# Preloading the final pass's constants and first spectrum, and storing repeated map rows one image later, in a two-layer spectral convolution kernel

## The reference

```python
# layer 0: spectral convolution, 4 heads of 16 channels
x_freq = rfft2(gn(x))
core = einsum('bhixy,hioxy->bhoxy', xf[..., :32, :17], weight[..., :32, :17])
x = x + irfft2(core placed in zeros) + bias
# layer 1: normalisation on the hyperboloid, over all images and pixels
m = mean of gn(x) over batch and pixels, one vector of 64 channels
mu = m / sqrt(max(m0^2 - sum(m[1:]^2), EPS))
alpha = max(x0 * mu0 - x[1:] @ mu[1:], 1 + EPS);  d = arccosh(alpha)
var = mean(d * d);  coef = d / sqrt(alpha^2 - 1)
v = coef * (x - alpha * mu);  vo = v - v0 / (1 + mu0) * (mu + e0)
s = gamma * vo[1:] / (sqrt(var) + EPS) + beta;  t = sqrt(1 + sum(s * s))
x = x + concat([t, s])
```

## Time and profile before

| | before |
|---|---|
| median of 3 runs | 3675.0 us (3665.37 to 3679.16) |
| the profiled execution's own time | 3669.49 us |
| its span | 3667.9 us |
| busy share PE, DVE, ACT, POOL | 80%, 75%, 57%, 41% |
| mean granted TensorE clock | 0.886 of full speed |
| DMA | 1211.32 MB, mean 330 GB/s |

### The profile page before, as it was taken

One profiled execution on the slowest core, in us unless ns is written; L12 is line 12 of the kernel. 1 busy time (PEld: TensorE's weight loads), 2 busy tenths in 40 slices (PEclk: granted clock), 3 DMA queues, 4 the chain that ended last, 5 costly groups with the idle time before them and its releaser, 6 DMA issues. The chain is left out here.

```text
span 3667.9 us, 70122 instructions
## 1 busy us (share of the span) xinstructions
PE 2923.4 (80%) x26018; PEld 1461.4 (40%) x26018; DVE 2747.2 (75%) x2984; ACT 2096.8 (57%) x2866; POOL 1512.5 (41%) x862
## 2 busy tenths in 40 slices
PE   6998888989843766776775498898888899888887
PEld 3555555555521221222221344444444444444443
DVE  1888888888886546544564398888888888888888
ACT  5776676767720011101111388787777787777787
POOL 0101011010111111111111287787777777777778
PEclk9998888988866888887787699999999999999999
DMA  9877767777716989999996599999999999999998
GB/s 379 298 265 258 277 244 290 258 277 274 248 64 224 400 326 391 400 397 387 403 399 221 177 391 382 380 376 374 371 368 368 368 378 376 370 381 373 370 386 341
DMA packets 293210, 1211.32 MB, mean 330 GB/s; under 512 B 35266, under 2 KB 49799, under 8 KB 210695
## 3 DMA queue, kind: packets, MB, share of 16 engines
q1 hardware_dynamic: 263526, 1152.42, 82.5%
q0 software_dynamic: 14112, 43.37, 3.6%
q10 hardware_dynamic: 15360, 12.60, 1.2%
HBM read 883.89 MB, written 324.31 MB: 329 GB/s over the span
## 5 line engine op out<-in xcount | busy, mean ns | idle before, releaser
L1309 POOL TENSOR_TENSOR c_ot<-c_ot,c_pp 128x1024 f32<-128x1024 f32 x512 | 1213.6, 2372 | 411.2 <-DVE c_ot L1262 410.0
L1252 DVE SCALAR_TENSOR_TENSOR c_xt<-c_xt,keep_k,c_p_u 128x1024 f32<-128x1024 f32 x512 | 653.7, 1277 | 135.8 <-PE c_p_u L1132 109.5
L1262 DVE SCALAR_TENSOR_TENSOR c_ot<-c_p_f,keep_k,c_xt 128x1024 f32<-128x1024 f32 x512 | 657.3, 1284 | 108.3 <-DMA out<-c_ot 59.8
L1206 ACT ACTIVATE c_pp<-c_p_p,keep_cols 128x1024 f32<-128x1024 f32 x512 | 570.7, 1115 | 259.8 <-PE c_p_p L1144 258.7
L1132 PE MATMUL c_p_u<-c_mv,c_zc 64*128 64x256 f32 x4096 | 595.6, 410 | 78.9 <-DVE c_xt L1252 76.9
L1213 ACT ACTIVATE c_sq<-c_xt,keep_cols 128x1024 f32<-128x1024 f32 x512 | 583.1, 1139 | 63.9 <-DVE c_xt L1252 63.6
L330 ACT ACTIVATE a_junk<-a_xt 128x1024 bf16<-128x1024 f32 x512 | 537.1, 1053 | 29.1 <-DMA a_xt<-in_x 21.8
L249 PE MATMUL a_p_rows<-a_xt,a_dft_h 128*64 128x512 f32 x2048 | 516.3, 650 | 32.8 <-DMA a_bias_t<-in_bias 18.1
L1132 PEld LDWEIGHTS c_p_u<-c_mv,c_zc 64*128 64x128 f32 x4096 | 361.1, 190 | 362.7 <-issue 219.5
L528 POOL TENSOR_TENSOR a_sm<-a_sm 128x8 f32<-128x8 f32 x16 | 26.7, 1670 | 929.4 <-DVE a_sm L463 929.4
L1144 PE MATMUL c_p_f<-c_rt,keep_lw 64*128 64x512 bf16 x1024 | 315.3, 388 | 104.6 <-DVE c_ot L1262 95.8
(11 more groups left out here) (206 smaller groups left out, 2964.1 us busy)
## 6 DMA issues: line engine op xcount, KB each, us to landing
a_xt<-in_x SPq DMA_DIRECT2D x256, 1024.0 KB, 8.1
b_xt<-in_x SPq DMA_DIRECT2D x128, 2048.0 KB, 16.8
c_xt<-in_x SPq DMA_DIRECT2D x256, 1024.0 KB, 15.9
out<-c_ot SPq DMA_DIRECT2D x256, 1024.0 KB, 16.3
c_rt<-maps SPq DMA_DIRECT2D x256, 96.0 KB
maps<-b_maps ACTq DMA_DIRECT2D x192, 64.0 KB, 13.7
maps<-b_maps POOLq DMA_DIRECT2D x64, 192.0 KB, 10.0
dmap<-b_dmap POOLq DMA_DIRECT2D x16, 768.0 KB, 13.2
```

The lines of the kernel that those rows point to most:

```text
L1206: S.activation(pp[n][:], p_p[:], ACT.Identity, bias=keep["cols"][:, b, 1:2]).then_inc(pp_done, 1)
L1252: V.scalar_tensor_tensor(out=u, in0=u, scalar=kc, in1=p_u[:], op0=ALU.mult, op1=ALU.add).then_inc(u_done, 1)
L1262: V.scalar_tensor_tensor(out=ot[t % NB][:, at], in0=p_f[:], scalar=kinv, in1=xt[t % NB][:, at], op0=ALU.add, op1=ALU.mult).then_inc(f_done, 1)
L1309: P.tensor_tensor(o, o, pp[n][:], ALU.add).then_inc(o_done, 1)
```

## The change

In the second pass ACT's order becomes copy_z(b), repeat_maps(b-1), distances(b), with the last image's stores at the end. At the end of the second pass SP waits until DVE has done `combine` for all images, and loads image 0's spectrum, `idft_c` and the cosine table into tiles that are now in `keep`. The table in HBM is 64 rows high and four times as wide, so one load of 64 rows fills half of a `mv` tile, and `mv` is not zeroed any more. The kept `ys` tile also serves as DVE's scratch (`v1`, `v2`) at the start of the second pass; two memsets of the upper halves of `ys` and `idft` follow there, ahead of `dense(0)`. `misc` is loaded once. In the final pass TensorE and ACT wait for the PSUM bank's memset alone (`filled` 1) and the preload's semaphores; `hw` is awaited only before the first `sums`. The `rt` tiles are zeroed by DVE (two) and POOL (two), and SP issues the first two x tiles before it waits for them.

```diff
@@ -70,11 +70,11 @@
     scale = np.where(ky == 0, 1.0, 2.0)[:, None] / N
-    iw = np.zeros((48, W))
+    iw = np.zeros((64, W))
...
     iw[M2 + 2] = 1.0
-    c["idft_w"] = iw
+    c["idft_w"] = np.tile(iw, (1, 4))
@@ -586,7 +586,7 @@
         xt = [sb(f"xt{k}", [128, TB]) for k in range(NX)]
-        misc = sb("misc", [128, 24])
+        misc = keep["misc"]
@@ -599,7 +599,8 @@
         ac, lc, q2, q3, dsum = sb("ac", [128, B]), sb("lc", [128, B]), sb("q2", [128, B]), sb("q3", [128, B]), sb("dsum", [128, B])
-        v1, v2 = sb("v1", [128, B, C]), sb("v2", [128, B, C])
+        ys_flat = keep["ys"][:].rearrange("p c m -> p (c m)")
+        v1, v2 = (ys_flat[:, B * C * k:B * C * k + B * C].rearrange("p (b c) -> p b c", c=C) for k in range(2))
@@ -637,7 +638,7 @@
             sp.dma_start(idft_h[0:64], cst["idft_d"]).then_inc(c_in, 16)
-            sp.dma_start(idft_w[:], cst["idft_w"][0:YS]).then_inc(c_in, 16)
+            sp.dma_start(idft_w[:], cst["idft_w"][0:YS, 0:W]).then_inc(c_in, 16)
@@ -650,6 +651,14 @@
                     load(b, t)
+            sp.wait_ge(v_ready, 3 * B)
+            sp.wait_ge(uw_out, 16)
+            for half in range(2):
+                load_modes_0(sp, keep, spec, half)
+            sp.dma_start(keep["idft"][0:64].rearrange("p a b c -> p (a b c)"), cst["idft_c"]).then_inc(keep["pre_in"], 16)
+            for m in keep["mv"]:
+                for at in range(2):
+                    sp.dma_start(m[64 * at:64 * at + 64], cst["idft_w"]).then_inc(keep["pre_in"], 16)
@@ -743,13 +752,15 @@
                 copy_z(b)
+                repeat_maps(b - 1)
                 distances(b)
-                repeat_maps(b)
...
             act.wait_ge(setup, 4)
-            entry(0)
+            copy_z(0)
+            distances(0)
...
                 entry(b)
+            repeat_maps(B - 1)
@@ -958,6 +969,8 @@
             combine(1)
+            ch.inc(V.memset(keep["ys"][64:128], 0.0))
+            ch.inc(V.memset(keep["idft"][64:128], 0.0))
@@ -984,6 +997,12 @@
+def load_modes_0(sp, keep, spec, half):
+    for k in range(2):
+        sp.dma_start(keep["ys"][KX * k:KX * k + KX, 32 * half:32 * half + 32].rearrange("k (h i) m -> k h (i m)", h=2),
+                     spec[0, k].rearrange("(h k) n -> k h n", h=HEADS)[:, 2 * half:2 * half + 2]).then_inc(keep["ys_in"][half], 16)
@@ -999,8 +1018,8 @@
     r_in = [sem(f"r_in{k}") for k in range(NB)]
-    ys_in = [sem(f"ys_in{k}") for k in range(2)]
-    c_in, zeroed, filled = sem("c_in"), sem("zeroed"), sem("filled")
+    ys_in, pre_in = keep["ys_in"], keep["pre_in"]
+    zeroed, filled = sem("zeroed"), sem("filled")
@@ -1013,15 +1032,14 @@
         rt = [sb(f"rt{k}", [128, TC], BF16) for k in range(NB)]
-        mv = [sb(f"mv{k}", [128, 4 * W]) for k in range(NB)]
+        mv = keep["mv"]
         zc = [sb(f"zc{k}", [128, 32, 2 * C]) for k in range(2)]
-        ys = sb("ys", [128, C, YS])
+        ys = keep["ys"]
...
         arg, th, o0 = (sb(n, [128, 512]) for n in ("arg", "th", "o0"))
-        idft = sb("idft", [128, 2, 2, 64])
-        misc = sb("misc", [128, 24])
+        idft, misc = keep["idft"], keep["misc"]
@@ -1030,8 +1048,6 @@
         def _(sp):
-            sp = Sync(sp, c_in)
@@ -1089,17 +1105,10 @@
-            sp.wait_ge(zeroed, 2 * NB + 1)
-            for half in range(2):
-                load_modes(0, half)
-            sp.dma_start(idft[0:64].rearrange("p a b c -> p (a b c)"), cst["idft_c"]).then_inc(c_in, 16)
-            sp.dma_start(misc[:], cst["misc"]).then_inc(c_in, 16)
-            for m in mv:
-                for at in range(2):
-                    sp.dma_start(m[64 * at:64 * at + 48].rearrange("p (r w) -> p r w", w=W), cst["idft_w"].unsqueeze(1).to_broadcast((48, 4, W))).then_inc(c_in, 16)
...
                 load_x(0, t)
-            sp.wait_ge(c_in, 16 * (2 + 2 * NB))
+            sp.wait_ge(pre_in, PRE_IN)
+            sp.wait_ge(zeroed, NB)
@@ -1149,8 +1158,11 @@
                 pe.wait_ge(sq_done, b * GR + 2 * t + 2)
-                if t == 0 and not is_at(b, 0):
-                    pe.wait_ge(t_read, b)
+                if t == 0:
+                    if is_at(b, 0):
+                        pe.wait_ge(filled, 2)
+                    else:
+                        pe.wait_ge(t_read, b)
@@ -1173,8 +1185,8 @@
-            pe.wait_ge(c_in, 16 * (2 + 2 * NB))
-            pe.wait_ge(filled, 3)
+            pe.wait_ge(pre_in, PRE_IN)
+            pe.wait_ge(filled, 1)
@@ -1229,8 +1241,7 @@
-            act.wait_ge(zeroed, 2 * NB + 1)
-            act.wait_ge(filled, 3)
+            act.wait_ge(filled, 1)
@@ -1281,15 +1292,10 @@
-            for r in rt:
-                V.memset(r[:], 0.0).then_inc(zeroed, 1)
-            for m in mv:
-                V.memset(m[:], 0.0).then_inc(zeroed, 1)
-            V.memset(ys[:], 0.0).then_inc(zeroed, 1)
-            V.memset(idft[64:128], 0.0).then_inc(filled, 1)
...
             V.memset(hw[:], 0.0).then_inc(chain, 1)
-            dve.wait_ge(c_in, 16 * (2 + 2 * NB))
+            for r in rt[:2]:
+                V.memset(r[:], 0.0).then_inc(zeroed, 1)
@@ -1321,10 +1327,14 @@
+            for r in rt[2:]:
+                P.memset(r[:], 0.0).then_inc(zeroed, 1)
...
+
+PRE_IN = 16 * 9
@@ -1341,7 +1351,10 @@
             keep = {"lw": sb("lw", [128, B, C, 2], BF16), "cols": sb("cols", [128, B, 2]),
-                    "k": sb("k", [128, 4])}
+                    "k": sb("k", [128, 4]), "ys": sb("ys", [128, C, YS]), "idft": sb("idft", [128, 2, 2, 64]),
+                    "misc": sb("misc", [128, 24]), "mv": [sb(f"mv{k}", [128, 4 * W]) for k in range(4)],
+                    "ys_in": [ctx.enter_context(nc.semaphore(f"ys_in{k}")) for k in range(2)],
+                    "pre_in": ctx.enter_context(nc.semaphore("pre_in"))}
```

## The result

| | before | after |
|---|---|---|
| median | 3670.6 us (4 runs, 3665.4 to 3679.2) | 3796.4 us (4 runs, 3791.5 to 3800.0) |
| profiled execution, its span | 3667.9 us | 3797.5 us |
| busy share PE, DVE, ACT, POOL | 80, 75, 57, 41% | 78, 72, 55, 40% |

The changed kernel is slower: ratio 1.0339, 95% interval 1.0312 to 1.0367, or 126 us. In the profiled executions it is 129.6 us.

The account below looks back on a forecast made before the run. The second pass was taken as bound by both full DMA engines and a DVE-POOL loop. Terms +146 + 2.3 - 8 - 25.8 = +114.5 on 3669.5 gave 3784 us, range 3635 to 3840.

Parts of the forecast that it names:

- turn = 29.2 + D: Second pass, from one `dense` to the next: 29.2 us plus D, rising from 51.7 to 63 us, +146 over 13 turns.
- D: Time of POOL's queue from first map store to the spectrum's landing; forecast to rise from 22 to 34 us.
- the turning point: The D, put at 24.4 us, at which 13 longer turns lose the 31.5 us that the seams give.
- the seams: Effects outside the 13 turns: +2.3 us before the loop, -8 at the second pass's end, -25.8 at the final pass's start.
- The head start of POOL's stores: Second pass: POOL's stores start 0 to 5 us before x loads resume, saving 0 to 8 us of D.
- TensorE's new wait: Second pass: TensorE stands for `combine` instead of ACT's copy, some 15 us an image.
- s + 40 and s + 62: Times after s, the start of `dense(b-1)`: the next image's tile 5 lands, and its row transform can start.
- The end of the pass: End of the second pass: `dense(15)` starts 32 us after `dense(14)`, not 39.6, held by ACT's last stores: -8 us.
- The preload: Loads at the second pass's end cost 0; the final pass's first transform starts 25.8 us earlier.
- A: Rival: bytes bound the second pass, so D stays at 22 and the turn at 51.7; 3638 or 3626 us; chance 0.16.
- B: Rival: ACT's copy still falls behind something long enough for x loads to pause as now; 3638 us; chance 0.06.
- C: Rival: x loads resume late, TensorE staying at 1.2 GHz; D is 25 to 26, 3681 us; chance 0.08.

Follow-up runs that it names:

- experiment 4: Changed kernel with each x tile of the second pass loaded by four transfers, so x packets are 4 KB and not 16 KB: 3633.6 us, ratio 0.985.
- experiment 10: Changed kernel with ACT's old order, the preload kept, and x tiles in four transfers: 3626.7 us, ratio 0.985.
- experiment 6: Changed kernel with POOL's queue reordered, the next spectrum's load issued ahead of the map stores: 3655.7 us, ratio 0.993.
- experiment 3: Changed kernel, but SP issues an image's fourth x tile only when that image's spectrum has landed: 3643.9 us, ratio 0.988.
- experiment 5: Changed kernel with each x tile in two transfers, so x packets are 8 KB: 3660.4 us, ratio 0.995.
- experiment 1: Changed kernel with ACT's old order (distances, then the stores of the same image), the preload kept: 3625.1 us, ratio 0.983.
- 9: Changed kernel with ACT's old order, the preload kept, and the second pass's two memsets moved behind the last dense: 3631.8 us, ratio 0.988.

## Why the prediction was right

The time (3784 forecast, 3796 measured) and the way to it were right. Some of the closeness is luck: the parts missed by +17.2, +3.9, -2.1, +0.4 and -4.2 us, and the last of these is chance.

- *The loop, turn = 29.2 + D.* It holds in the changed kernel (64.3 = 29.2 + 35.1) and, where POOL's queue keeps its order and x packets are 8 KB or more, within 0.2 us in the variants: 51.5 with 22.2, 53.2 with 24.0, 54.7 with 25.5. With quarters it holds for the first turns (49.3 with 20.1), but over all 13 they are 2.1 us longer in experiment 4 and 1.4 in experiment 10, where TensorE waits for x and the DMA engines are full. By the same formula I should have put the turning point at a D of 25.0 and not 24.4, for the 31.5 us of the seams are 2.4 a turn and a turn of 51.7 has a D of 22.5. Moving the load off the loop (experiment 6) broke it.
- *D rises because x loads don't pause.* Forecast 34, measured 35.1 over the 13 turns. Shown from both sides by pausing them (experiment 3) and by shrinking their packets (4 and 5), with ACT's order, the stores and the bytes left alone. They do still pause in some turns, but at the start of D and not at its end.
- *The head start of POOL's stores.* This is the term that was mis-sized. I took 4 us off the undisturbed 38, at 2.5 us of work for each us alone. D came out at 35.1, 3 us below 38. In the turn from 1552.95 x loads stood for some 6 us at the start of D, by my price worth 9, and D was still 34.6: only 0.56 MB went through in them, while in a usual turn of the kernel before 1.92 MB went through from 1883 to 1892 us, when all of POOL's transfers had been issued. Here the largest store was issued at 1575.28 and the spectrum's load at 1576.28, after the pause. So by these rows not only the length of a pause counts, but also whether the queue is already filled when it comes; no experiment moved the pause alone. The 1.1 us by which D was missed are 15 of the 17 us; the rest comes from rounding the turn of 63.2 to 63.
- *TensorE's new wait.* 15 us an image forecast, 15.8 measured; the old one fell to 2 us. The working agrees less well than the number: s + 40 and s + 62 would give 19 us after tile 5's own 3.4, and in the turn from 1552.95 tile 5 landed at s + 47 and the wait was 11.2; in the turn before it was 25.3.
- *The end of the pass.* -8 forecast, -10.1 measured, and `dense(15)` waits for ACT's stores, as forecast. In this pass I named that wait only at its end; that it would be the next bound everywhere, once the spectrum was out of the way, I learnt from experiment 6.
- *The preload.* The 25.8 us came to the tenth, with the maps' loads issued 19 us early; POOL's two memsets took 3.54 us. The transfers at the end of the second pass cost nothing that shows.
- *Missed.* +6.2 and not +2.3 up to `dense(1)`: 2.0 of it before the memsets, 1.4 in a longer first turn. The 2.0 is within what varies: with the preload `combine(1)` begins at 1205.2 to 1208.4 us in these profiles. I had priced the memsets as a delay alone; experiments 1 and 9 show that such a delay can also decide which of two patterns the first turns take, 14.6 us at `dense(14)`.

The rivals failed at their premises. A's full DMA engines were a sign of two limits at one place, and the share fell to 0.88 when the loop grew. A was right in one thing: with smaller packets, or with the added buffer, the engines are full again (1.01 to 1.03), and no variant has a turn under 50.3 us. Against B, the copy does come early: TensorE's wait for it is 18.4 us in all. C wanted a D of 25 to 26, and no turn has less than 33.0.

## What to carry to other kernels

When a wait is removed on one engine, look at which queue it had kept quiet and who profited; full DMA engines don't say that the bytes are the only bound, if a small transfer on a dependency loop shares them with a stream of large ones. Compute the length of each closed loop, one in which every step waits for the one before and the first for the last, with its transfers at the duration that they have beside the stream, not alone. The remedies are to issue the small transfer early, to cut the stream into smaller packets, or to give the loop one more buffer; here they brought 136 to 177 us back, and the next loop showed up at once.

## What was not expected of the hardware

- The size of one queue's packets sets how long another queue takes: 35.3, 25.6 and 19.4 us for the same 2.45 MB beside x packets of 16, 8 and 4 KB. The price is small: alone on the engines the x stream moves 4.33 MB in 10 us with the large packets and 4.10 with the small ones.
- The queues went packet for packet, whatever the packets hold: 534, 519 and 487 packets carried 7.96, 1.89 and 0.40 MB in the same 29 us.
- A pause of the large stream helped POOL's queue less while its large transfers were not yet issued: 0.56 MB went through in 6 us at the start of D in the changed kernel, 1.92 MB in 9 us late in D in the kernel before. No run changed that alone.
- ACT's issue of its twelve transfers varies. It takes 5.6 to 5.8 us in most turns of the kernel before and in experiment 1, but 13.8 in the turn at 1300 us, where the x queue was nearly empty and POOL's had 56.1%; 6 to 11 in the changed kernel; and 7 to 15 in experiment 5, for instance 14.9 at 1674 us beside 54.9% of x and 34.4% of POOL's queue. So it doesn't take an empty x queue. Quick stores of POOL go with the slow turns, but don't explain them alone: in experiment 4 the issue at 1497 us takes 5.8 us beside 48.6% of POOL's queue. The cause was not tried.
